# Earlier combining, a later wait and a denser last median in a wavelet, convolution and median kernel

## What is computed

```python
cA, cH, cV, cD = dwt2(x)                       # Haar bands, 16 x 16 each
proc = lambda c: batchnorm_relu(einsum('bchw,oc->bohw', c, conv_w), bn_gamma, bn_beta)
rimg0 = idwt2(proc(cA), proc(cH), proc(cV), proc(cD))
rimg1 = ...                                    # three levels of dwt2 and back: equals x
y = conv3x3(concatenate([rimg0, rimg1], axis=1), convW_w) + convW_b   # 256 -> 128 channels
x1 = batchnorm_relu(y, bnW_gamma, bnW_beta)
med = median_of_3x3(x1)                        # zero padding
out = x1 + einsum('bchw,oc->bohw', med, W) + b
```

## Time and profile of the kernel before

| | |
|---|---|
| median of 3 runs | 421.12 us (420.78 to 421.69) |
| the profiled execution's own time | 423.23 us |
| its span, first to last instruction | 421.3 us |
| busy share of the span | PE 94%, DVE 91%, PE weight loads 50%, POOL 46%, ACT 36% |
| mean granted TensorE clock | 0.987 |

### The profile page before, as it was taken

The page is one execution under the profiler, slowest core; times in us unless marked ns, Lnnn a source line. Parts: engine busy times, 40 slices in busy tenths (PEclk is TensorE's granted clock), DMA queues, the critical chain, the costliest instruction groups (busy, mean ns, idle before and its releaser), DMA issues.

```text
span 421.3 us, 3650 instructions
## 1 busy us (share of the span) xinstructions
PE 397.0 (94%) x1119; PEld 210.2 (50%) x1120; DVE 383.4 (91%) x532; ACT 152.8 (36%) x348; POOL 194.5 (46%) x194
## 2 busy tenths in 40 slices
PE   7889999999999999999999999999999967997875
PEld 2335588846444444444444444444455856862331
DVE  3899857999849999999999999999999999999974
ACT  2465763412262423324141414232233211249820
POOL 3999395713443552637344444536272700006700
PEclk9999999999999999999999999999999996999989
DMA  7970200100101101010110101010100000002656
GB/s 280 418 322 3 96 4 2 50 0 2 51 0 50 51 0 51 0 50 0 51 50 1 50 0 52 0 50 1 50 0 2 0 1 2 0 0 100 249 205 246
DMA packets 7796, 26.72 MB, mean 63 GB/s; under 512 B 992, under 2 KB 1248, under 8 KB 7776
## 3 DMA queue, kind: packets, MB, share of 16 engines
q1 hardware_dynamic: 7776, 26.48, 16.6%
HBM read 18.09 MB, written 8.39 MB: 63 GB/s over the span
## 4 chain that ended last, share of the span: by engine, by line
PE 62%; DVE 21%; POOL 7%; issue 7%; DMA 2%; ACT 1%; SPq 0%; POOLq 0%; DVEq 0%
PE conv_ps L381 55%; DVE y L914 3%; PE one_ps L363 3%; PE one_ps L446 2%; PE conv_ps L469 2%; POOL y L212 2%; POOL y L213 2%; DMA ru<-x 2%; DVE one_ps L842 1%; DVE sorted_cols L838 1%; DVE sorted_cols L794 1%; DVE sorted_cols L834 1%; DVE sorted_cols L790 1%; DVE z L823 1%; DVE one_ps L821 1%
## 5 line engine op out<-in xcount | busy, mean ns | idle before, releaser
L381 PE MATMUL conv_ps<-ru,wt 128*128 128x512 f32 (+1 forms) x360 | 132.4, 504 | 0.0
L381 PEld LDWEIGHTS conv_ps<-ru,wt 128*128 128x128 f32 x360 | 69.1, 192 | 53.6 <-issue 50.1
L381 PE MATMUL conv_ps<-xu,wt 128*128 128x496 f32 (+3 forms) x240 | 89.2, 509 | 6.2 <-DVE conv_ps L757 6.2
L569 ACT ACTIVATE y<-conv_ps,sgn 128x512 f32<-128x512 f32 (+1 forms) x40 | 25.5, 637 | 170.8 <-PE conv_ps L381 170.8
L381 PEld LDWEIGHTS conv_ps<-xu,wt 128*128 128x128 f32 x240 | 46.7, 195 | 42.3 <-issue 33.2
L219 POOL TENSOR_TENSOR ru<-z 128x512 f32<-128x512 f32 x14 | 17.9, 1276 | 83.7 <-DVE one_ps L827 83.2
L381 PE MATMUL conv_ps<-ru,v 128*128 128x496 f32 (+3 forms) x120 | 43.9, 501 | 0.3 <-POOL ru L220 0.3
L381 PE MATMUL conv_ps<-y,v 128*128 128x496 f32 (+3 forms) x108 | 38.6, 491 | 0.0
L381 PE MATMUL conv_ps<-y,wt 128*128 128x496 f32 (+3 forms) x108 | 38.6, 491 | 0.0
L469 PE MATMUL conv_ps<-z,w 128*128 128x512 f32 x64 | 31.8, 640 | 6.0 <-DVE y L914 6.0
L318 POOL TENSOR_TENSOR ru<-eo 128x512 f32<-128x512 f32 x16 | 17.0, 1060 | 43.3 <-PE conv_ps L381 42.8
(11 more groups left out here) (128 smaller groups left out, 646.6 us busy)
## 6 DMA issues: line engine op xcount, KB each, us to landing
raw<-x SPq DMA_DIRECT2D x20, 512.0 KB, 3.3
out<-y SPq DMA_DIRECT2D x15, 512.0 KB, 2.6
ru<-x SPq DMA_DIRECT2D x8, 512.0 KB, 9.0
xu<-x SPq DMA_DIRECT2D x4, 512.0 KB, 9.0
wt<-w_t SPq DMA_DIRECT2D x2, 576.0 KB, 10.7
out<-y SPq DMA_DIRECT2D x2, 256.0 KB, 3.2
w<-w_t SPq DMA_DIRECT2D x2, 64.0 KB, 4.6
vec<-vectors SPq DMA_DIRECT2D x1, 3.0 KB, 9.7
```

The source lines that it names most:

```text
L381: return nc.tensor.matmul(bank(u, b)[:, (r0 - row) * BW:(r1 - row) * BW], taps(half, kx, ky), plane[:, (r0 + dy) * BW:(r1 + dy) * BW], sta ...
L569: S.activation(at(slot(n), row * W + b, [[2, cols]]), src, ACT.Identity, scale=sgn[:, :], accum_out=y_sum[:, part:part + 1]).then_inc(y_ke ...
```

## The change

Three edits. The median combines early also where image n+2 is one of `HALVED`, that is in images 12 and 13 (and in all of `HALVED` as before). On POOL, L318 and L319 wait for `rows_read` of image n-2 in place of `y_done`; the wait for `rows_read` that stood ahead of `make_xu03` goes, as it would come after. `FINISH_AT` becomes steps 15 to 28, so that fourteen finishes instead of nine lie within the last two medians, two of them (15 and 16) in the last but one.

```diff
-    BN3_AT, FINISH_AT = 8, (17, 18, 20, 21, 22, 24, 25, 27, 28)
+    BN3_AT, FINISH_AT = 8, tuple(range(15, 29))
...
                 else:
-                    pool.wait_ge(y_done, 2 * (last_unit(n - 2) + 1))
+
+                    pool.wait_ge(rows_read, last_unit(n - 2) + 1)
...
                 make_ru03(n)
-                pool.wait_ge(rows_read, last_unit(n - 2) + 1)
                 make_xu03(n)
...
-                early, late = (seeds, None) if n in HALVED else (None, seeds)
+                early, late = (seeds, None) if n in HALVED or n + 2 in HALVED else (None, seeds)
```

## The result

The changed kernel takes 419.01 us in the median of 7 runs (418.10 to 420.07), the kernel before 421.18 us (420.67 to 423.64): ratio 0.9936, 95% interval 0.9913 to 0.9959. The prediction was 419.2 us with a range of 417.0 to 420.6. The profiled execution of the changed kernel has a span of 417.1 us and an own time of 418.86. That is 4.2 us of span less than in the profile of before, about twice what the medians differ by; the profile of before lies 2 us above its median, this one at its median. So the two traces tell where time went, and the runs tell how much.

What follows compares the result with a forecast made beforehand. Bounds: PE at 154, DVE from 314 to 404, then the chain behind the last median. Terms of -0.2 us up to the batch norm and -1.7 after made -1.9 from 421.12, so 419.2 us, range 417.0 to 420.6.

Steps and rivals of the forecast that it cites:

- The POOL wait: L318, L319 moved behind the reading of the rows: L784, L785 shorten in image 12's median, minus 1.03 us.
- PE's wait: At 154.17, PE's idle time for POOL's row sums goes: minus 0.34 us, up to 0.6.
- margin ahead of L817: POOL's four moved-back instructions end before L817 with 0.3 to 0.4 us to spare; a miss costs at most 0.84 per median.
- The early combining: Images 12 and 13: costs DVE 0.46 us; PE's 6.23 us idle nearly goes, about 5.2 us appears before `outputs(19)`.
- The drains: L838 to L842 and L842 to L846, images 12 and 13: 0.23 us longer per median, plus 0.46 in all.
- 0.7 us given back to the clock: Before the second batch norm: `outputs(19)` loses 2.3 us at low clock (bounds 0 and 3.0), so the norm gains only 0.2.
- The finishes: Fourteen instead of nine before the last median's end: median ends 5.9 us later, tail minus 1.7 us (minus 0.6 to 3.7).
- collisions: Last median's two-SBUF-input instructions against POOL's `map_x1`: one fewer, minus 0.7 us, range 0 to minus 1.4.
- The output DMAs: At the end: they follow the last finish as before, 3.66 us to the span's end, no change.
- (a): Rival: clock holds in both gaps or falls too late to matter; 417.2 us, 416.5 with collisions gone; chance 0.2.
- (b): Rival: POOL misses its margin and `outputs(19)` loses 3.0 us, 421.2; or L784, L785 stay slow, 420.6; chance 0.13 together.
- (c): Rival: at finishes 2 to 13, late low-clock mixes hold the last median; four turn -1.9 into +0.9, 422.0 us; chance 0.05.

Runs made afterwards that it cites:

- the last experiment on POOL: Changed kernel with L311 and L312 on POOL also put behind the reading of the rows: 424.58 us, ratio 1.0075 to the kernel before.

## Why the prediction was right, step by step

**The POOL wait: right, mechanism and size.** 1.03 us at image 12 is what the trace gives. PE's wait was mis-sized: I took the 0.34 us that the row shows as idle, and named 0.6 as its upper end; it was 0.61 (0.60 with the edit alone), as the group behind the wait also started slower. The 0.34 us of margin ahead of L817 was real, and the last experiment on POOL shows the price of missing it. By the rule of the Trainium skill (SBUF — State Buffer, "Who interferes with whom") the shared port is an exclusive lock, and the first to start keeps it. These rows agree that the two engines collide there, but not that one simply waits for the other: L819 lost 0.23 us of the 0.32 that L322 still had, and behind it the instructions lengthen on both engines (1.50 us instead of 0.69 on DVE, 1.46 and 1.43 instead of 1.01 and 0.99 on POOL). The measurement decides; how the port is shared between them is not shown.

**The early combining: right that it costs, right about why, only partly in its shape.** The drains were 0.52, not 0.46. That the one harmless gap would become two, the second of them in front of the batch norm, is what the traces show. What failed is the step in which the first, short gap was passed over: in the profiled execution the clock fell behind it, at 356.3, made `outputs(18)` end 1.8 us later and so shortened the second gap to 3.28 us, where it is 4.97 with the clock held; then it fell again. `outputs(19)` took 6.86 us to the zeros behind it instead of 5.08, a loss of 1.8 where I had taken 2.3. The kernel with zeros ahead of the last mix was traced in this case, too (gaps of 2.30 and 3.29 us). In the other two traces of the changed kernel and in the one with this edit alone the second case is seen: one low stretch of about 7 us, mostly in `outputs(19)`, a loss of 2.9, 2.8 and 3.1 us where I had 3.0 as the bound, and a wait of 1.30, 1.16 and 1.48 us. So my 0.7 us given back to the clock was a middle value between two cases, and each of these five traces has one or the other. The experiments put the whole edit at a loss of about 1 us.

**The finishes: right in sum, with two errors that offset each other.** 1.57 us against the 1.7 predicted. Nearly two collisions went, not one: L784 of the last median takes 0.46 us instead of 1.13, and L817 0.73 instead of 1.18, 0.27 over its undisturbed 0.46. L784 before and, in the second fence, in the changed kernel:

```profile
381.96 1.13 DVE L784 TENSOR_TENSOR one_ps<-y 128x288 f32<-128x288 f32 x1
```

```profile
382.78 0.46 DVE L784 TENSOR_TENSOR one_ps<-y 128x288 f32<-128x288 f32 x1
```

The last median's L846 is followed by ACT's norm at 408.11, 34.55 us after the norm began against 29.67 before: 4.9 instead of 5.6. Finishes waited about 0.15 us in sum and not 0.4. Against that, the last mix was at the low clock from end to end, and from its start to DVE's last start it took 4.23 us, where I had 3.4 to 3.84.

**The output DMAs: wrong.** I had costed them at nothing. The end of the span says otherwise: before, the last three finishes stood in one group of 2.83 us, so 1 MB went out nearly at once. From 417 to 419.5 the DMA engines were busy without a break, the last two transfers took 3.2 us to land, and the span ended 3.66 us after the last finish. With finish 14 brought forward they took 2.1 us, and the span ended after 2.47 us. The kernels divide the same way: 3.66, 3.73 and 3.67 us with nine finishes, 2.4 to 2.5 with fourteen, and 2.7 where the zeros bring the two halves to 1.2 us from each other. The term that I missed, 1.2 us, is as large as the 1.1 us that I had allowed the tail to be weaker than forecast.

Why, then, was 419.2 so near 419.01? In part by luck. The traces' sum would be -0.61 - 1.03 + 0.52 + 0.25 - 1.57 - 1.19 = -3.6 us with the short wait and about -2.6 with the long one, and the three sets of runs gave -2.1 to -3.2. My sum lacked the DMA term and was too low for PE's wait by 0.3; that the timed runs gain somewhat less than the traces, as with the POOL wait alone (0.8 for 1.5) and the zeros, made up for it. I had also taken for granted that every term read from an execution 2.1 us above the median holds in the median one. Traces of one kernel show how unlike its executions are, be it by chance or by the chip: the changed kernel's spans are 417.1, 419.1 and 419.2 us, and about 1 us of that lies ahead of 151 us and another 1 us in the wait for the squares. Which of the kernel's executions a trace happens to catch thus decides as much as an edit does, and the difference between runs and traces is not explained further here.

Of the rivals: (a), the clock holding in both gaps, was seen in no trace. (b) didn't occur; its part with `outputs(19)` losing nearly 3.0 us did, in two of the three traces of the changed kernel. (c) didn't: but for the last one, the mixes of the changed kernel ran at 1.00, with waits of about 0.2 us between them. The rule that I set beside it (the Trainium skill, TensorE: Matmul & The Clock Gate, "A second HAM failure mode") tells of a clock that falls again and again between groups of matmuls. No trace here shows that; the nearest is one fall, with the early combining alone and nine finishes, where the clock lay at 0.50 from 386.8 to 390.2 behind a gap of 1.91 us. Behind a gap of 1.89 us at the same place the kernel before kept 1.00.

## What to carry to other kernels

Where an engine's instructions with two SBUF inputs stand in order of time, look for the stretch whose instructions have at most one SBUF input and put GpSimd's work there; count its length against that stretch, because 0.3 us of margin was enough and 2.5 us more of work cost 6 us. Releasing work earlier is no gain when its engine must then wait somewhere else: a gap is harmless or not by what stands behind it, and here moving one from a covered place to the front of a barrier cost about 1 us. That it also made the runs spread is not shown: the kernel before spreads by 2 to 5 us in a set without it. In a chain of last images, thin out what follows the last long computation: its finishes, its DMAs in flight, and the idle of the engine that does the last product.

## What was not expected of the hardware

- TensorE's clock fell after a gap of only 2.30 us (0.50 from 356.3, with PE at work since 355.04), and in another execution of the same kernel it held through the same gap and fell during the next, of 4.97 us. The same program takes either way. Its times spread over 2.0 to 3.4 us in a set; how much of that is the clock is not shown, as its traces differ by 1 us ahead of 151 us already.
- With VectorE and GpSimd both reading SBUF in instruction after instruction, both slowed down: 128x512 took 1.50 us instead of 0.69 on VectorE, and 128x480 took 1.46 us instead of 1.01 on GpSimd.
- Twenty bf16 matmuls of zeros were enough to hold the clock at 1.00 through the 4.1 us (405.7 to 409.8) in which the kernel had nothing else for PE to do.
- The end of the span followed the last finish by 2.4 us with the last two DMAs 2.1 us apart, 2.7 us at 1.2 us apart, and 3.7 us where another 512 KB were issued right ahead of them.
